# Stages joined without barriers, norm moments merged by group, and the normalising on ScalarE

## The chip, the cores and the metric

The kernel runs on one core of a Trainium2 chip. Its engines are TensorE (PE in the profile, its weight loads PEld), VectorE (DVE), ScalarE (ACT), GpSimd (POOL) and SyncE (SP), which issues DMAs. Each works through its own instructions in order and waits on semaphores for the others. The metric is the device time of one execution in microseconds (us).

## The reference

The input is x of 2048 tokens by 128 channels. Eight residual steps follow each other, and each first applies a layer norm without weights:

```
x = x + attn_softmax(_layernorm(x))      # 16 heads of 8, causal
x = x + channel_mix(_layernorm(x))       # sigmoid(xr Wr) * (relu(xk Wk)^2 Wv)
x = x + gated_linear(_layernorm(x))      # kv_t = k_t * kv_(t-1) + (1 - k_t) * v_t
x = x + channel_mix(_layernorm(x))       # the same weights again
x = x + retention(_layernorm(x))         # fixed decay for each head, group norm, Wo
x = x + experts(_layernorm(x))           # 8 experts, top 2
x = x + lightning(_layernorm(x))         # fixed decay, layer norm, gate, Wo
x = x + experts(_layernorm(x))

def _layernorm(x, axis=-1, eps=1e-05):
    m = jnp.mean(x, axis=axis, keepdims=True)
    v = jnp.var(x, axis=axis, keepdims=True)
    return (x - m) / jnp.sqrt(v + eps)
```

In channel mixing xr and xk are mixtures of a token with the one ahead of it.

## The kernel before

x stays in SBUF as 16 tiles of 128 tokens by 128 channels. Four tiles are a group or chunk of 512 tokens (NC = 4 chunks of TPC = 4 tiles). Normed tiles are transposed on TensorE and copied to xT, channels by tokens, which the products read.

**Order of work.** Every engine's instructions are written out by hand and run in that order; there is no scheduler. Each stage is an nc.Block, and a barrier of all engines lies between two Blocks. The program is: the attention, project_out, channel_mix "f0", linear_attention "g" (gated), channel_mix "f1", end_stage, linear_attention "r" with retention_out, experts "m0", linear_attention "l" with lightning_out, end_stage, experts "m1". end_stage is a Block of its own in which GpSimd clears the semaphores, so that two barriers lie around it.

**Norm.** VectorE takes statistics of each tile of x (bn_stats, L201) as soon as the tile's sum is ready, in the stage ahead. At the start of the next stage seven small VectorE operations merge them for all 16 tiles (L159 to L165), GpSimd raises the variances to the power -1/2, one instruction for each group (L178), VectorE normalises four tiles for each group (L170), TensorE transposes them (L189), and ScalarE copies them out of PSUM (L196). TensorE first issues 12 products whose result nobody reads (unread, L136).

**Channel mixing.** For each chunk GpSimd takes the difference with the shifted tokens (L968), VectorE forms xk and xr (L948, L950), TensorE multiplies (L1000, L1005, L992), ScalarE applies relu, square and sigmoid (L977 to L981), and VectorE gates the product, adds it to x and takes the statistics (L957, L960, L201). TensorE ends with 12 more unread products.

**Linear attention.** 32 steps n, eight for each chunk c, e = n % 8. In a step TensorE spreads the values over the rows (L1269) or a DMA does it, an update is formed on VectorE (L1139) or, in 9 of the steps, on GpSimd (L1109), VectorE scans the recurrence (L1156), GpSimd multiplies the state by q (L1104), and TensorE sums the result four steps later (L1249, L1254). ScalarE takes k and q for each chunk, and in "lightning" it also applies silu to each value (L1207). In "gated" VectorE adds a finished chunk to x in the next one (L1115, L1117), otherwise ScalarE copies it (L1172) and VectorE takes its statistics.

**Experts.** After the norm the gate's logits are made (L1721) and copied (L1536); a long VectorE chain sorts the tokens, and a loop of 39 tiles follows. At the end VectorE adds the weighted results to x, chunk by chunk.

## Time and profile before

| | us |
|---|---|
| median of three runs | 1173.02 |
| lowest and highest run | 1171.45, 1174.34 |
| the profiled execution | 1179.64 |
| its span in the trace | 1177.9 |

Busy time in the span: TensorE 1009.3 us, VectorE 808.1, ScalarE 510.3, GpSimd 432.2. The attention takes the first 491 us. The stages behind it follow each other in the trace: output product from 491.5, f0 from 500.4, g from 527.4, f1 from 605.1, r from 633.5, its output from 704.9, m0 from 718.0, l from 899.6, its output from 978.7, m1 from 997.0.

A row of a timeline reads: start in us, duration in us, engine, line, operation, output and input with their shapes, count, and in brackets how long the engine had stood idle before it and what ended that. Rows of one group that follow each other at once are merged, and the duration is then of all of them. A row of busy time by stretch reads: stretch, its length, then for TensorE, its weight loads, VectorE, ScalarE and GpSimd the busy us and the count, then TensorE's granted clock (1.00 is 2.4 GHz, 0.50 is 1.2 GHz), the DMA share and GB/s.

### The profile page before, as it was taken

The page shows a single profiled execution, that of the slowest core. Times are in us where ns is not written, and L with a number is a line of the kernel's source. Part 1 is how long each engine was busy: PE and PEld are TensorE (multiplying, and loading weights), DVE is VectorE, ACT ScalarE, POOL GpSimd, SP SyncE. Part 2 cuts the span into 40 slices and gives each one's busy share as a digit, 9 for nine tenths or more (in the row PEclk, how much of TensorE's full clock was granted, in tenths as well). Part 3 has the DMA queues.
Part 4 walks back from the last instruction along what each step waited for, and adds up shares of the span by engine and source line. Part 5 has one row for each costly group of instructions (what it writes and reads, how often), then busy time and mean ns, then how long its engine had stood idle before and what let it go on. Part 6 is the DMA issues. An engine that isn't in the chain of part 4 may idle for free. (4 is left out here: it accounts for less than half of the span.)

```text
span 1177.9 us, 18330 instructions
## 1 busy us (share of the span) xinstructions
PE 1009.3 (86%) x6327; PEld 523.2 (44%) x6327; DVE 808.1 (69%) x1504; ACT 510.3 (43%) x1048; POOL 432.2 (37%) x506
## 2 busy tenths in 40 slices
PE   5587899999999999879868976899994996799993
PEld 3232322322222332456645424566662664566662
DVE  6886989999889780288987976533337786733335
ACT  5344577588777677532113102133334431133333
POOL 3320110011011111137862871266652785156661
PEclk9598999999999899979979997999996997899997
DMA  6753500000000000242100201011112210111114
GB/s 127 173 97 55 108 2 2 1 2 2 1 1 2 2 2 2 95 125 70 52 1 10 80 18 36 14 43 42 44 36 81 63 36 1 36 39 41 43 41 122
DMA packets 50207, 51.50 MB, mean 44 GB/s; under 512 B 7668, under 2 KB 39804, under 8 KB 50108
## 3 DMA queue, kind: packets, MB, share of 16 engines
q1 hardware_dynamic: 45128, 40.11, 13.7%
q0 software_dynamic: 4992, 10.23, 3.2%
q8 instruction: 54, 0.88, 0.3%
q14 instruction: 33, 0.27, 0.1%
HBM read 33.22 MB, written 16.91 MB: 43 GB/s over the span
## 5 line engine op out<-in xcount | busy, mean ns | idle before, releaser
L731 DVE TENSOR_REDUCE mpart<-ps 128x2 f32<-128x1024 f32 (+3 forms) x320 | 324.7, 1061 | 48.0 <-PE ps L782 30.6
L859 ACT ACTIVATE arena<-ps 128x512 f32<-128x512 f32 (+3 forms) x640 | 291.7, 542 | 133.1 <-PE ps L799 132.6
L799 PE MATMUL ps<-arena 51*128 51x512 bf16 (+3 forms) x640 | 175.6, 357 | 13.2 <-DMA arena<-mrow 5.8
L813 PE MATMUL ps<-arena,w 128*32 128x512 f32 (+3 forms) x1280 | 154.2, 554 | 2.7 <-ACT arena L859 2.2
L782 PE MATMUL ps<-arena 51*128 51x512 bf16 (+3 forms) x640 | 141.7, 361 | 13.2 <-DVE mpart L731 5.8
L701 POOL TENSOR_SCALAR_AFFINE_SELECT arena<-arena 128x512 f32<-128x512 f32 x64 | 40.8, 637 | 300.1 <-ACT arena L859 230.1
L1697 ACT ACTIVATE arena<-ps 128x512 f32<-128x512 f32 x78 | 46.6, 598 | 214.7 <-PE ps L1763 200.2
L1104 POOL TENSOR_TENSOR arena<-arena 128x512 f32<-128x512 f32 x96 | 121.1, 1274 | 42.4 <-DVE arena L1156 42.1
L799 PEld LDWEIGHTS ps<-arena 51*128 51x128 bf16 x640 | 49.3, 94 | 167.5 <-ACT arena L859 131.1
L1156 DVE TENSOR_TENSOR_SCAN arena<-ps,arena 128x512 f32<-128x512 f32 x96 | 118.3, 1253 | 0.4 <-POOL arena L1109 0.4
L1607 DVE COPY arena<-ps 128x128 f32<-128x128 f32 x78 | 22.8, 292 | 135.8 <-PE ps L1753 96.9
L1662 POOL DMA_INDIRECT results<-arena x78 | 77.2, 989 | 88.5 <-DVE arena L1624 77.8
L1651 POOL DMA_INDIRECT arena<-tokens,arena x78 | 75.9, 973 | 75.1 <-DVE arena L1600 52.0
L136 PE MATMUL ps<-cstb 128*128 128x320 bf16 x324 | 57.9, 344 | 39.2 <-PEq L1491 18.4
L1762 PE MATMUL ps<-w,arena 128*128 x156 | 81.7, 605 | 3.1 <-DVE arena L1607 2.6
L1781 PE MATMUL ps<-w,arena 128*128 x624 | 82.7, 275 | 1.1 <-DVE arena L1624 1.1
L1763 PE MATMUL ps<-w,arena 128*128 x156 | 79.7, 592 | 0.0
L1781 PEld LDWEIGHTS ps<-w,arena 128*128 128x128 f32 x624 | 75.8, 192 | 1.6 <-issue 1.5
L1269 PE MATMUL ps<-xt,arena 128*128 128x512 f32 x138 | 70.4, 598 | 0.7 <-DVE arena L1139 0.7
L178 POOL TENSOR_TENSOR small<-small,neghalf 128x4 f32<-128x4 f32 x32 | 32.5, 1054 | 95.0 <-DVE small L165 95.0
L1139 DVE TENSOR_TENSOR arena<-ps,arena 128x512 f32<-128x512 f32 x69 | 46.7, 678 | 25.6 <-ACT ps L1207 13.4
L196 ACT COPY xt<-ps 128x512 f32<-128x512 f32 x28 | 16.2, 591 | 110.6 <-PE ps L189 110.5
(267 smaller groups left out, 1479.4 us busy)
## 6 DMA issues: line engine op xcount, KB each, us to landing
w<-in_w SPq DMA_DIRECT2D x2, 2048.0 KB, 10.9
arena<-results SPq DMA_DIRECT2D x16, 256.0 KB, 5.0
arena<-q_stack SPq DMA_DIRECT2D x8, 384.0 KB
arena<-k_stack SPq DMA_DIRECT2D x8, 384.0 KB
arena<-g_v SPq DMA_DIRECT2D x9, 256.0 KB, 3.9
arena<-r_v SPq DMA_DIRECT2D x9, 256.0 KB, 3.6
arena<-l_v SPq DMA_DIRECT2D x9, 256.0 KB, 3.6
tokens<-arena SPq DMA_DIRECT2D x8, 256.0 KB, 2.4
```

The source lines that it names most:

```text
L731: nc.vector.tensor_reduce(out=mpart[:, 2 * pl:2 * pl + 2, t, kc], in_=ps[:, bank:bank + 2, 0:width], axis=AX.X, op=ALU.max).then_inc(ring_ ...
L782: ins = nc.tensor.matmul(ps[:, bank + side, 0:width], rows(Qs, side, 2 * g + pl, (c * TPC + t) * P, (c * TPC + t + 1) * P), rows(Ks, side, ...
L799: nc.tensor.matmul(ps[:, n % ST, off:CH], rows(Ks, j % 2, 2 * g + j // 2, kt * P, (kt + 1) * P), rows(Qs, j % 2, 2 * g + j // 2, c * CH + ...
L813: ins = nc.tensor.matmul(ps[32 * j:32 * j + 32, O, off:CH], vg[kt // (NT // 2)][:, kt % (NT // 2), g * GH + j, :], probs[:, u % 2, j, off: ...
L859: nc.scalar.activation(probs[:, n % 2, j[0], off:CH], ps[:, (GH * n + j[0]) % ST, off:CH], ACT.Exp, scale=float(HD) ** -0.5).then_inc(exp_ ...
L1104: nc.gpsimd.tensor_tensor(z[:, n % ZB, :], state[:, n % SB, :], q[:, c % 2, :], ALU.mult).then_inc(z_ready, 1)
L1156: nc.vector.tensor_tensor_scan(out=state[:, n % SB, :], data0=a, data1=upd[n % UB], initial=0.0 if c == 0 else state[:, (n - HD) % SB, CH ...
L1651: nc.gpsimd.indirect_dma_start(out=xs[:, s, :], out_offset=None, in_=token_rows, in_offset=bass.IndirectOffsetOnAxis(ap=gather_row[:, s:s ...
L1662: nc.gpsimd.indirect_dma_start(out=result_rows, out_offset=bass.IndirectOffsetOnAxis(ap=result_row[:, s:s + 1], axis=0), in_=y[:, s % YB, ...
L1762: nc.tensor.matmul(ps[:, i % 2, :], xsT[:, i % 2, :], w1[:, expert[i], :], start=True, stop=True)
L1763: nc.tensor.matmul(ps[:, 2 + i % 2, :], xsT[:, i % 2, :], w3[:, expert[i], :], start=True, stop=True).then_inc(up_ready, 1)
L1781: ins = nc.tensor.matmul(ps[:, 7, 0:D], hidT[:, s % 2, f, :], w2[:, expert[s], f, :], start=f == 0, stop=f == NF - 1)
```

## The change

All that follows the attention is written as Stage objects, which run joins into two Blocks: the first from project_out to retention_out, the second from experts "m0" to experts "m1". One end_stage lies ahead of the first Block, one between the two. Inside a Block each engine goes on with its part of the next stage.

- The merge of the moments is done for each group of four tiles (merge), by VectorE in the stage ahead, right behind the statistics of that group (x_statistics with the norm that follows). Only for "m0" all four merges stand at its own start. In the gated loop the statistics of a chunk now stand right behind its add.
- GpSimd makes power and product of minus mean and power for a group (two instructions), and ScalarE normalises with them (normalise), in one queue with its copies: normalise 0, normalise 1, copy 0, normalise 2, copy 1, normalise 3, copy 2, copy 3.
- In linear attention group 3 is normalised, transposed and copied within step 2 of the recurrence. GpSimd's copies of the weights stand between the powers of groups 1 and 2. Transposes use the banks 1, 5, 1, 7.
- The unread products ahead of each norm and at the end of channel mixing are gone. Those in the experts stay.
- In lightning_out the sigmoids of the gate stand behind the normalising of groups 0 to 2, and that of group 3 between them.

```diff
+            def merge(self, dve, g):
+                if self.link is None:
+                    self.link = Chain(dve, self.chain)
+                link, o = self.link, slice(4 * g, 4 * g + 4)
...
+            def gpsimd(self, pool, groups):
+                for g in groups:
+                    o = slice(4 * g, 4 * g + 4)
+                    pool.wait_ge(self.var_ready, g + 1)
+                    nc.gpsimd.tensor_tensor(small[:, 5, o], small[:, 4, o], neghalf[:, 0:4], ALU.pow).then_inc(self.powered, 1)
+                    pool.wait_ge(self.powered, g + 1)
+                    nc.gpsimd.tensor_tensor(small[:, 6, o], small[:, 0, o], small[:, 5, o], ALU.mult).then_inc(self.rstd_ready, 1)
+
+            def normalise(self, act, g):
+                act.wait_ge(self.rstd_ready, g + 1)
+                for t in range(4 * g, 4 * g + 4):
+                    ins = nc.scalar.activation(self.dst[:, t, :], self.src[:, t, :], ACT.Identity, bias=small[:, 6, t:t + 1],
+                                               scale=small[:, 5, t:t + 1])
+                ins.then_inc(self.normed, 1)
...
-            def tensor(self, pe, groups=None):
-                if groups is None or groups[0] == 0:
-                    unread(self.banks[1], 12)
...
+                last = statistics(range(c * TPC, (c + 1) * TPC), x)
+                if norm is None:
+                    return
+                last.then_inc(norm.chain, 1)
+                norm.link = norm.link or Chain(dve, norm.chain)
+                norm.link.n += 1
+                dve.wait_ge(norm.chain, norm.link.n)
+                norm.merge(dve, c)
...
-                    value(NC - 1)
-                    unread(0, 12)
...
+                    if n == 2:
+                        norm.normalise(act, 3)
+                        norm.copy(act, 3)
...
+            def scalar(act):
+                for g in (0, 1, 2):
+                    norm.normalise(act, g)
+                for c in range(NC):
+                    if c == 2:
+                        norm.normalise(act, 3)
+                    o = slice(c * CH, (c + 1) * CH)
+                    nc.scalar.activation(gate[:, o], gate[:, o], ACT.Sigmoid).then_inc(gate_ready, 1)
...
+        run([attended, mixed, gated, mixed_again, retained, retention_out("r", y, z, None)])
         end_stage()
...
+        run([chosen, lightened, lightened_out, chosen_again])
```

VectorE, from the last chunk of f0's mixing to the first scans of "g", in the kernel before:

```order
L957 TENSOR_TENSOR arena<-ps,arena 128x512
L960 TENSOR_TENSOR x<-arena,x 128x512
L201 BN_STATS stats<-x 128x6 x4
L941 UNCONDITIONAL_BRANCH
L1127 UNCONDITIONAL_BRANCH
L159 TENSOR_TENSOR small<-stats 128x16
L160 TENSOR_TENSOR small<-stats 128x16
L161 TENSOR_TENSOR small<-stats 128x16
L162 TENSOR_TENSOR small<-small 128x16
L163 TENSOR_SCALAR small<-small 128x16
L164 TENSOR_SCALAR small<-small 128x16
L165 SCALAR_TENSOR_TENSOR small<-small 128x16
```

The same place in the changed kernel, where L974 and L977 are what L957 and L960 were:

```order
L974 TENSOR_TENSOR arena<-ps,arena 128x512
L977 TENSOR_TENSOR x<-arena,x 128x512
L212 BN_STATS stats<-x 128x6 x4
L161 TENSOR_TENSOR small<-stats 128x4
L162 TENSOR_TENSOR small<-stats 128x4
L163 TENSOR_TENSOR small<-stats 128x4
L164 TENSOR_TENSOR small<-small 128x4
L165 TENSOR_SCALAR small<-small 128x4
L166 TENSOR_SCALAR small<-small 128x4
L167 SCALAR_TENSOR_TENSOR small<-small 128x4
L1156 TENSOR_TENSOR arena<-ps,arena 128x512 x2
L1173 SCALAR_TENSOR_TENSOR arena<-ps,arena 128x512
```

The seven operations stand behind every group's statistics, three times more within the mixing, and the normalising is gone from VectorE; the updates follow at once.

ScalarE, from the end of f1's mixing into the retention recurrence, before (L977 to L981 are the mixing, L196 the norm's copies, L1187 and L1195 k and q, L1212 the values for the DMA):

```order
L977 ACTIVATE arena<-ps 128x512
L979 ACTIVATE arena<-arena 128x512
L981 ACTIVATE arena<-ps 128x512
L941 UNCONDITIONAL_BRANCH
L1174 UNCONDITIONAL_BRANCH
L196 COPY xt<-ps 128x512 x2
L1187 COPY arena<-ps 128x512
L1195 ACTIVATE arena<-ps 128x512
L196 COPY xt<-ps 128x512 x2
L1212 ACTIVATE xn<-ps 128x512
```

And in the changed kernel (L181 normalises a tile, L197 copies):

```order
L998 ACTIVATE arena<-ps 128x512
L181 ACTIVATE xn<-x,small 128x128 x8
L197 COPY xt<-ps 128x512
L181 ACTIVATE xn<-x,small 128x128 x4
L197 COPY xt<-ps 128x512
L1204 COPY arena<-ps 128x512
L1212 ACTIVATE arena<-ps 128x512
L197 COPY xt<-ps 128x512
L1236 ACTIVATE xn<-ps 128x512
L181 ACTIVATE xn<-x,small 128x128 x4
L197 COPY xt<-ps 128x512
```

Twelve tiles are now normalised ahead of k and q, and four more in the recurrence, behind the first copy of values.

TensorE at the same border, before (L1000, L1005 and L992 are the mixing, L136 the unread products, L189 transposes, L1238 k and q, L1269 and L1277 values):

```order
L992 MATMUL ps<-w_wv,arena 128x128 x8
L136 MATMUL ps<-cstb 128x320 x12
L941 UNCONDITIONAL_BRANCH
L1227 UNCONDITIONAL_BRANCH
L136 MATMUL ps<-cstb 128x320 x12
L189 MATMUL ps<-cst,xn 128x128 x8
L1238 MATMUL ps<-xt,w_rk 128x512
L1238 MATMUL ps<-xt,w_rq 128x512
L189 MATMUL ps<-cst,xn 128x128 x8
L1269 MATMUL ps<-xt,arena 128x512 x2
```

And in the changed kernel:

```order
L1008 MATMUL ps<-w_wv,arena 128x128 x8
L192 MATMUL ps<-cst,xn 128x128 x8
L1266 MATMUL ps<-xt,w_rk 128x512
L1266 MATMUL ps<-xt,w_rq 128x512
L192 MATMUL ps<-cst,xn 128x128 x4
L1299 MATMUL ps<-xt,arena 128x512 x2
L1307 MATMUL ps<-xt,w_rv 128x512
```

The unread products are gone from both sides of the border, and the transposes of the last group come later.

## Rows read from the trace of the kernel before

**Rows 1.** Busy time by stretch, the lightning recurrence from its fourth step.

```profile
916.00:977.50 61.50, 58.68 (x313) 38.98 (x311) 48.28 (x60) 20.82 (x36) 48.10 (x39) 1.00 0.13 39
```

**Rows 2.** Timelines of VectorE, GpSimd and ScalarE, prologue of the attention.

```profile
3.78 0.87 DVE L472 BATCH_NORM_STATS2 xstats<-x 128x6 f32<-128x128 f32 x4 [2.82 <-DMA x<-in_x]
...
9.84 0.86 DVE L472 BATCH_NORM_STATS2 xstats<-x 128x6 f32<-128x128 f32 x4
...
11.51 0.87 DVE L472 BATCH_NORM_STATS2 xstats<-x 128x6 f32<-128x128 f32 x4
...
5.64 1.04 POOL L432 TENSOR_TENSOR small<-small,neghalf 128x4 f32<-128x4 f32 x1 [5.13 <-DVE small L466]
...
6.99 1.65 ACT L584 ACTIVATE xn<-x,small 128x128 f32<-128x128 f32 x4 [4.90 <-POOL small L434]
```

**Rows 3.** Timeline, VectorE's first add of the attention's output product.

```profile
494.03 0.69 DVE L918 TENSOR_TENSOR x<-ps,x 128x512 f32<-128x512 f32 x1 [2.83 <-PE ps L900]
```

**Rows 4.** Timeline, norm and first channel mixing.

```profile
504.88 4.07 DVE L170 TENSOR_SCALAR xn<-x,small 128x128 f32<-128x128 f32 x7
...
510.32 2.08 PE L1000 MATMUL ps<-arena,w_wk 128*128 128x512 f32 x2 [0.20 <-DVE arena L950]
...
516.96 0.69 DVE L957 TENSOR_TENSOR arena<-ps,arena 128x512 f32<-128x512 f32 x1 [1.91 <-PE ps L992]
...
523.70 0.87 DVE L201 BATCH_NORM_STATS2 stats<-x 128x6 f32<-128x128 f32 x4
...
524.50 0.67 DVE L957 TENSOR_TENSOR arena<-ps,arena 128x512 f32<-128x512 f32 x1
```

**Rows 5.** Timeline, gated linear attention: start, third scan, a wait.

```profile
532.75 2.08 POOL L1097 COPY arena<-w_hv 128x128 f32<-128x128 f32 x8
...
540.99 1.21 DVE L1156 TENSOR_TENSOR_SCAN arena<-ps,arena 128x512 f32<-128x512 f32 x1
...
577.21 0.69 DVE L1139 TENSOR_TENSOR arena<-ps,arena 128x512 f32<-128x512 f32 x1 [1.73 <-PE ps L1269]
```

**Rows 6.** Timeline, gated end, second mixing, end_stage, third retention scan.

```profile
602.43 0.69 DVE L1115 TENSOR_TENSOR x<-ps,x 128x512 f32<-128x512 f32 x1 [2.80 <-PE ps L1254]
...
615.00 2.07 PE L1000 MATMUL ps<-arena,w_wk 128*128 128x512 f32 x2 [0.21 <-DVE arena L950]
...
622.20 0.69 DVE L957 TENSOR_TENSOR arena<-ps,arena 128x512 f32<-128x512 f32 x1 [2.47 <-PE ps L992]
...
633.55 0.19 DVE L159 TENSOR_TENSOR small<-stats 128x16 f32<-128x16 f32 x1 [1.52 <-PEq L74]
...
646.97 1.21 DVE L1156 TENSOR_TENSOR_SCAN arena<-ps,arena 128x512 f32<-128x512 f32 x1
```

**Rows 7.** Timeline, start of the first experts.

```profile
718.00 0.17 DVE L1494 MEMSET arena<- 128x128 f32 x1 [0.36 <-PEq L1335]
...
720.65 4.22 DVE L170 TENSOR_SCALAR arena<-x,small 128x128 f32<-128x128 f32 x16 [1.13 <-POOL small L178]
...
727.89 0.69 DVE L1536 COPY arena<-ps 128x512 f32<-128x512 f32 x1 [2.92 <-PE ps L1721]
```

**Rows 8.** Timeline, lightning recurrence: third scan, GpSimd's last products.

```profile
914.31 1.21 DVE L1156 TENSOR_TENSOR_SCAN arena<-ps,arena 128x512 f32<-128x512 f32 x1
...
971.97 3.71 POOL L1104 TENSOR_TENSOR arena<-arena 128x512 f32<-128x512 f32 x3
```

**Rows 9.** Timeline, lightning output and start of the second experts.

```profile
976.93 0.59 ACT L1172 COPY arena<-ps 128x512 f32<-128x512 f32 x1 [8.31 <-PE ps L1254]
...
978.69 1.28 ACT L1412 ACT_TABLE_LOAD   x1 [1.17 <-PEq L1089]
...
1006.95 0.69 DVE L1536 COPY arena<-ps 128x512 f32<-128x512 f32 x1 [2.94 <-PE ps L1721]
```

**Rows 10.** Busy time by stretch, TensorE's clock at the second mixing's start.

```profile
605.00:607.00 2.00, 1.79 (x12) 1.10 (x12) 0.89 (x7) 0.00 (x0) 0.90 (x1) 1.00 0.00 0
...
610.00:613.00 3.00, 1.13 (x5) 0.71 (x4) 3.00 (x5) 1.18 (x2) 3.00 (x4) 0.50 0.00 0
```

More of the change, by code:

```diff
@@ L185, in tensor @@
+            def normalise(self, act, g):
[4 more added lines that the diff above has]
+                ins.then_inc(self.normed, 1)
+            def tensor(self, pe, groups=range(4)):
+                for g in groups:
                     pe.wait_ge(self.normed, g + 1)
[L186 to L187 removed]
+                    before = [h for h in range(g) if self.banks[h] == self.banks[g]]
+                    if before:
+                        pe.wait_ge(self.out, before[-1] + 1)
@@ new lines, in tensor @@
+            def tensor(pe):
+                norm.tensor(pe)
+                for c in range(NC):
+                    pe.wait_ge(gated, c + 1)
+                    if c >= 2:
+                        pe.wait_ge(added, c - 1)
+                    for t in range(TPC):
+                        ins = nc.tensor.matmul(ps[:, 2 + c % 2, t * P:(t + 1) * P],
+                                               xT[:, c * CH + t * P:c * CH + (t + 1) * P], w["lo"][:], start=True, stop=True)
+                    ins.then_inc(product, 1)
@@ L1437, in experts @@
+            return Stage(vector=vector, scalar=scalar, gpsimd=gpsimd, tensor=tensor)
+        def experts(name, token_rows, result_rows, norm, following):
+            last = following is None
             at = [0]
@@ L1785, in build @@
+                    for stage in stages:
+                        if stage.sync:
+                            stage.sync(sp)
         softmax_attention()
-        channel_mix("f0")
-        linear_attention("g", "gated")
-        channel_mix("f1")
         end_stage()
-        linear_attention("r", "retention")
-        experts("m0", tokens[0], results[0], last=False)
-        linear_attention("l", "lightning")
-        end_stage()
-        experts("m1", tokens[1], results[1], last=True)
+        LINEAR_BANKS = (1, 5, 1, 7)
```

1378 lines of the change are left out of this document (689 added, 689 removed).

## The prediction

> **What bounds the kernel now.** I read the timeline around each border of stages first, then the busy time by stretch, then the lines of the long loops. The change does not touch the attention, which fills the first 491 us, nor the long expert loops; it touches six borders and three recurrences. At a border no engine is full. Work passes from one to the next: VectorE's last add and statistics, the merge of the moments, GpSimd's power, a normalising engine, TensorE's transposes, ScalarE's copy. So a border is priced by the length of that chain, and a queue that one engine is in order by. The barriers themselves are small: VectorE stands 0.36 us at a plain one and 1.52 us where end_stage lies between two [rows 6, 7]. In the lightning recurrence TensorE is busy 58.7 of 61.5 us and VectorE 48.3, GpSimd 48.1 [rows 1]; in the gated one VectorE has a wait of up to 1.73 us once in a chunk of some 16 us [rows 5].
>
> **Prices of the new pieces.** The prologue of the attention already works in the new way, by groups of four tiles [rows 2]. VectorE's statistics begin at 9.84 and the next ones at 11.51: 1.67 us with a merge. In channel mixing the next operation starts 0.80 us after the statistics [rows 4]. A merge so costs VectorE 0.87 us for each group, where before one merge of about the same length did for 16 tiles. From the start of the statistics to the power it is 1.86 us (3.78 to 5.64), from the power to ScalarE 1.35 us (5.64 to 6.99; power and product on GpSimd), and ScalarE takes 1.65 us for four tiles. VectorE took 4.2 us for 16 [rows 7], so the normalising itself gets 2.4 us longer per norm, and it is in ScalarE's queue with the 0.6 us copies.
>
> **Border 1: output product, first channel mixing, gated start.** VectorE's adds begin at 494.03 [rows 3]; a group is then 0.73 + 0.80 + 0.87 = 2.40 us, the last power can start at 494.03 + 0.73 + 1.86 + 3 x 2.40 = 503.8, ScalarE normalises from 505.2 to 506.85, and transposes at 1.1 us let TensorE start the mixing at 508.0. Before it started at 510.32. From there to the first gated product it was 6.64 us (516.96) and I keep that, since ScalarE's table load and the low clock stay: 514.65. Then VectorE sets the pace, 0.72 + 0.73 + 0.80 + 0.87 = 3.1 us a group which is longer than what TensorE needs between two products there [rows 4]: powers from 517.95, 521.1, 524.2, 527.35. The gated start needs group 1 normalised (522.45 to 524.1) and copied (524.7); GpSimd puts 2.1 us of weight copies [rows 5] between the powers of groups 1 and 2, so ScalarE normalises group 2 till 527.8, copies, and makes decay and k (1.3 us) by about 529.7. TensorE's value products for steps 0 to 2 follow; that of step 3 stands behind the transposes of group 3, which wait for ScalarE's normalising in the loop. The third scan comes at 536.2 with a fast TensorE, 537.6 with a slow one, before 540.99 [rows 5]. With 1.2 us for the end_stage that now stands behind the attention: a gain of 2.7 us, bounds 1 to 4.
>
> **Gated loop.** Three merges (2.6 us) and one set of statistics (0.8 us) come into the loop, on VectorE's way. One wait of 1.73 us per chunk can swallow part [rows 5]. Loss 3.0 us, bounds 1.5 (half is swallowed) and 5 (TensorE and GpSimd stall behind it).
>
> **Border 2: gated end, second mixing, retention start.** TensorE's last products let VectorE add at 602.43 [rows 6]. By then groups 0 and 1 are nearly normalised; the last power starts at 602.43 + 0.73 + 0.73 + 1.86 = 605.75, and behind GpSimd's first difference at 606.6; ScalarE normalises group 3 from 608.0 to 609.65, transposes till 610.8. Before it was 615.00: 4.2 us. The first gated product comes 7.2 us later as before (622.20 to 618.0). Powers at 621.3, 624.4, 627.6, 630.7; end_stage is gone. The third scan, by the same steps as above, at 639 to 640.5, before 646.97. Gain 7.3, bounds 5 to 8.5.
>
> **Border 3: retention output, experts start.** The barrier ahead of the output gives 0.3 us back; end_stage costs 1.2 us more than the plain barrier did. From the first memset (718.00) to the copy of the logits it was 9.9 us [rows 7]. Now: 0.7 us to the first merge, power at 1.7, ScalarE from 3.0; normalise, normalise, copy, normalise, copy, normalise, copy, copy are 4 x 1.65 + 4 x 0.6 = 9.0 us in one queue, with a wait for the last transposes 9.6, then the logits 1.2: 13.8. Loss 3.9 + 1.0 = 4.9, bounds 3.5 and 5.3. What hid this before was that VectorE and ScalarE shared it.
>
> **Border 4: experts to lightning.** The tail of the experts is VectorE's: 4 merges of 0.87 less one end merge and a barrier. Power of the last group 2.6 us later than before, but the early groups are long normalised: scans could start 2.4 us sooner. Yet in step 2 ScalarE must normalise and copy group 3 (2.3 us) ahead of the value of step 3, and the third scan comes at 914.7 against 914.31 [rows 8]. Loss 0.3, bounds -1 and +1.
>
> **Lightning loop.** Three merges, 2.6 us, in a loop where VectorE has 13 us of waits [rows 1]. But the last merge stands ahead of the last scan while GpSimd works 3.71 us in a row [rows 8]. In the first mixing seven normalising operations took VectorE 4.07 us beside GpSimd's differences [rows 4], against 0.26 us each without them. If the merge waits in this way for two such operations, the last scan slips by 2.1 us, and the two before it by some 0.5 each. Loss 3.0, bounds 1 and 5. The Trainium skill, page "SBUF — State Buffer", section "Who interferes with whom", says that a VectorE instruction with two SBUF inputs contends with a GpSimd instruction that reads SBUF; statistics, with one input, do not. The trace agrees for the slow operations just named, and shows none of a merge in such a place; by the rule the merge pays, without it the loss is 1.
>
> **Border 5: lightning output, experts start.** ScalarE is free at 977.5 [rows 9]: three normalisings, a table load of 1.28, two sigmoids, the fourth normalising: 986.4; transposes and the scale and shift till 987.9, then the first product: VectorE's add at 989.65. Powers at 992.25 + 3 x 2.40 = 999.45, ScalarE 1000.8 to 1002.45, transposes and copy 1004.1, logits 1005.2. Before 1006.95 [rows 9]. Gain 1.8, bounds 0.5 and 3.5.
>
> **Sum.** 2.7 - 3.0 + 7.3 - 4.9 - 0.3 - 3.0 + 1.8 = +0.6 us gained. The profiled execution took 1179.64 us (span 1177.9), 6.6 over the median of the three timed runs; from 1179.64 to 1179.0, and on the median 1173.02 to 1172.4.
>
> **TensorE's clock.** The filler matmuls ahead of every norm and after each mixing are gone. They worked only partly: from 605 to 607 the filler had the clock at 1.00, from 610 to 613, after sparse transposes, it was 0.50, thus 1.2 GHz, and the first products of the mixing, 1.0 us each, ran so too [rows 6, 10]. A mixing so already starts slow, and my terms carry that. What is new is that the starts of the recurrences, which had it at 1.00 after 24 fillers, come after sparse transposes too. The Trainium skill, page "TensorE: Matmul & The Clock Gate", section "Why this matters for your kernels", advises against idle gaps between bursts; by it the change would lose, and the third rival prices that from rows.
>
> **Rivals.**
> First, *the cover holds* (faster): merges vanish in the waits of the loops (loop losses 1.5 and 1.0), and TensorE is fast at the borders (gains 3.5, 8.2, 2.8, losses 4.8 and 0.3). Sum 7.9: 1165. For it: VectorE's 13 us of waits. Against it: the place of the last merge.
> Second, *merges collide with GpSimd* (slower): each of six merges in loops waits for two operations of 1.25 us; the loops lose 5 + 5 instead of 6: 1176.5. It decides the sign when loops lose more than 8.2 us with the borders as above.
> Third, *the clock falls further* (slower): a product takes 2.07 us at 1.2 GHz [rows 6], some 1.0 us more than at 2.4. If one more chunk of three products runs so in each mixing, that is 3.1 us less about 0.5 of VectorE's surplus, twice 2.6; and each of three recurrence starts waits one such product more, with its transposes 1.3 us: 5.2 + 3.9 = 9.1 us, 1181.5. For it: clocks of 0.50 after sparse transposes. Against it: at 605 the clock was still 1.00 though TensorE had had nothing since 602.4 [rows 6, 10].
> That the change doesn't do what it says can be left out: its order shows the pieces.
>
> **How the numbers follow.** The forecast, 1172.4 with own range 1168 to 1177, has 0.40; the first rival 0.30; the second 0.13; the third 0.17. The range 1163.5 to 1181 leaves some 0.15 out. A difference under 0.3% (3.5 us) can't be told from none. Faster by more: nearly all of the first rival and a fifth of the forecast, 0.37. Slower by more: most of the third, three quarters of the second, a tenth of the forecast, 0.28. Within: 0.35.
>
> **What would show it.** In the new profile: a VectorE group of mixing at 3.1 us; the first scan of retention 8 us sooner relative to the gated end; 13.8 us from the experts' memset to the logits; the two loops longer by 3 us each; GpSimd's wait ahead of the last two products of lightning. I would be wrong if the clock in the mixings is at 1.00 from the start or at 0.50 throughout, or if a merge in a loop takes over 1.5 us or costs its loop nothing.

## The result, and the profile after

The changed kernel takes 1178.87 us (median of five runs, 1178.35 to 1180.21), the kernel before 1173.02 (five runs, 1171.45 to 1174.78). The ratio is 1.0051, 95% interval 1.0037 to 1.0066: slower by 5.9 us, where 0.6 us less was forecast. When the changed kernel was measured once more beside other runs of the kernel before, the ratio was 1.0036 (1.0014 to 1.0059).

The profiled execution took 1179.97 us, its span is 1178.2. Only 0.3 us separate it from the span of before, since the attention, which is the same code in both, ended 4.1 us earlier in it (VectorE's last operation there starts at 486.80 against 490.92). Over all the executions profiled for this study that time lies anywhere from 482.6 to 490.9. So the traces are compared from the attention's end on, and there the changed kernel takes 691.4 us against 687.0: 4.4 us longer. The table cuts these into intervals between starts of VectorE rows.

| interval | before | after | gained | forecast |
|---|---|---|---|---|
| attention's end to first add of the output product | 3.11 | 3.88 | -0.8 | -1.2 |
| first add to third gated scan | 46.96 | 41.95 | +5.0 | +3.9 |
| third gated scan to gated end (last add) | 61.44 | 67.76 | -6.3 | -3.0 |
| gated end to third retention scan | 44.54 | 36.15 | +8.4 | +7.3 |
| third retention scan to group norm | 57.93 | 58.25 | -0.3 | 0 |
| group norm to first memset of the experts | 13.10 | 14.34 | -1.2 | -1.0 |
| memset to copy of the logits | 9.89 | 14.09 | -4.2 | -3.9 |
| logits to first weighted add, first experts | 160.16 | 159.11 | +1.1 | 0 |
| weighted add to third lightning scan | 26.26 | 27.33 | -1.1 | -0.3 |
| third to fifth lightning scan | 3.86 | 6.62 | -2.8 | 0 |
| fifth lightning scan to last statistics | 59.38 | 63.38 | -4.0 | -3.0 |
| last statistics to logits of the second experts | 29.40 | 28.17 | +1.2 | +1.8 |
| logits to end of span | 170.95 | 170.37 | +0.6 | 0 |

Timeline of VectorE in the changed kernel: first add, first gated product, third gated scan, one operation of a merge in the gated loop, the loop's wait, an operation of the last merge in the loop, last gated add, first gated product of the second mixing, third retention scan, memset and copy of the logits at the experts.

```profile
490.68 0.69 DVE L937 TENSOR_TENSOR x<-ps,x 128x512 f32<-128x512 f32 x1 [3.58 <-PE ps L921]
...
511.27 0.69 DVE L974 TENSOR_TENSOR arena<-ps,arena 128x512 f32<-128x512 f32 x1 [1.55 <-PE ps L1008]
...
532.63 1.21 DVE L1173 TENSOR_TENSOR_SCAN arena<-ps,arena 128x512 f32<-128x512 f32 x1
...
558.13 0.16 DVE L162 TENSOR_TENSOR small<-stats 128x4 f32<-128x4 f32 x1
...
571.31 0.69 DVE L1156 TENSOR_TENSOR arena<-ps,arena 128x512 f32<-128x512 f32 x1 [1.74 <-PE ps L1299]
...
592.34 1.23 DVE L163 TENSOR_TENSOR small<-stats 128x4 f32<-128x4 f32 x1
...
600.39 0.69 DVE L1130 TENSOR_TENSOR x<-ps,x 128x512 f32<-128x512 f32 x1 [3.88 <-PE ps L1282]
...
615.82 0.69 DVE L974 TENSOR_TENSOR arena<-ps,arena 128x512 f32<-128x512 f32 x1 [2.76 <-PE ps L1008]
...
636.54 1.21 DVE L1173 TENSOR_TENSOR_SCAN arena<-ps,arena 128x512 f32<-128x512 f32 x1
...
709.13 0.17 DVE L1518 MEMSET arena<- 128x128 f32 x1 [1.56 <-PEq L74]
...
723.22 0.69 DVE L1562 COPY arena<-ps 128x512 f32<-128x512 f32 x1 [10.07 <-PE ps L1743]
```

These answer to [rows 3 to 7]. Borders 1 and 2 are what the steps said, or better, and border 3 is 0.5 us worse. The gated loop is far off: its wait of 1.73 us [rows 5] is still there, 1.74 us, so it has swallowed nothing of the new operations. TensorE's rows ahead of it in the changed kernel (L1282 sums, L1299 gives the value):

```profile
567.53 1.16 PE L1282 MATMUL ps<-arena 128*128 128x128 f32 x8 [1.29 <-POOL arena L1120]
...
570.25 1.02 PE L1299 MATMUL ps<-xt,arena 128*128 128x512 f32 x2
```

The value that VectorE waits for stands in TensorE's order behind sums that waited 1.29 us for GpSimd, and GpSimd multiplies what VectorE has scanned. The three engines take turns: when VectorE comes later, so do the others, and the wait is no slack.

Timelines of TensorE and VectorE at the start of the lightning recurrence in the changed kernel, and TensorE's busy time by stretch there (the sixth figure behind the length is the granted clock):

```profile
906.38 0.66 PE L192 MATMUL ps<-cst,xn 128*128 128x128 f32 x4 [2.21 <-ACT xn L181]
906.87 1.53 PE L1299 MATMUL ps<-xt,arena 128*128 128x512 f32 x2
908.33 2.07 PE L1316 MATMUL ps<-arena,w_lg 8*128 8x512 f32 x2
910.33 2.08 PE L1299 MATMUL ps<-xt,arena 128*128 128x512 f32 x2
```

```profile
904.47 1.21 DVE L1173 TENSOR_TENSOR_SCAN arena<-ps,arena 128x512 f32<-128x512 f32 x1
909.05 0.69 DVE L1156 TENSOR_TENSOR arena<-ps,arena 128x512 f32<-128x512 f32 x1 [3.37 <-ACT ps L1231]
909.66 1.21 DVE L1173 TENSOR_TENSOR_SCAN arena<-ps,arena 128x512 f32<-128x512 f32 x1
913.06 0.69 DVE L1156 TENSOR_TENSOR arena<-ps,arena 128x512 f32<-128x512 f32 x1 [2.19 <-ACT ps L1231]
```

```profile
904.00:907.00 3.00, 0.79 (x6) 0.62 (x6) 1.68 (x2) 2.12 (x5) 2.28 (x2) 1.00 0.24 76
907.00:910.00 3.00, 3.00 (x5) 0.56 (x3) 0.95 (x2) 1.17 (x2) 0.02 (x1) 0.54 0.58 193
910.00:913.00 3.00, 3.00 (x7) 1.64 (x7) 0.87 (x1) 1.14 (x2) 1.27 (x1) 0.50 0.00 0
```

TensorE stands idle for 2.21 us in front of the four transposes of group 3, which wait for ScalarE's normalising. Behind them come the values of step 3, which have nothing to do with group 3. Then the granted clock falls from 1.00 to 0.50, 1.2 GHz, and a value product, which is two rows of the trace, takes 2.08 us instead of 1.02. VectorE waits 3.37 and 2.19 us.

Timeline of VectorE at the end of the lightning loop in the kernel before, where the last scan began 0.77 us behind the start of the statistics:

```profile
971.92 0.85 DVE L201 BATCH_NORM_STATS2 stats<-arena 128x6 f32<-128x128 f32 x4
972.69 1.26 DVE L1156 TENSOR_TENSOR_SCAN arena<-ps,arena 128x512 f32<-128x512 f32 x1
```

And in the changed kernel, where it begins 3.11 us behind:

```profile
972.06 0.85 DVE L212 BATCH_NORM_STATS2 stats<-arena 128x6 f32<-128x128 f32 x4
972.94 0.44 DVE L161 TENSOR_TENSOR small<-stats 128x4 f32<-128x4 f32 x1
973.31 1.30 DVE L162 TENSOR_TENSOR small<-stats 128x4 f32<-128x4 f32 x1
...
975.17 1.28 DVE L1173 TENSOR_TENSOR_SCAN arena<-ps,arena 128x512 f32<-128x512 f32 x1
```

And GpSimd's rows at the same place, and at the merge at 592.34 of the gated loop:

```profile
592.28 1.26 POOL L1120 TENSOR_TENSOR arena<-arena 128x512 f32<-128x512 f32 x1
...
972.10 2.49 POOL L1120 TENSOR_TENSOR arena<-arena 128x512 f32<-128x512 f32 x2
```

An operation of four columns takes 1.23 or 1.30 us beside a GpSimd product of 1.25, and 0.16 without one (558.13 above). The last merge meets two products: its first operation, 0.44 us, ends with the first of them, its second with the second. The two earlier merges of the lightning loop have one operation each of 0.63 and 0.62 us; two of the three in the gated loop meet none.

### The profile page after: what moved, and what is told of

Read it like the earlier page. It is cut to its first block and busy times, and to the rows that moved or that the text cites. A ratio compares the mean times of both kernels' runs of the same rounds, so it can differ in the third digit from the quotient of the medians.

```text
span 1178.2 us, 18204 instructions
## 1 busy us (share of the span) xinstructions
PE 992.3 (84%) x6207; PEld 512.7 (44%) x6207; DVE 795.5 (68%) x1544; ACT 558.7 (47%) x1176; POOL 439.6 (37%) x538
## 5 line engine op out<-in xcount | busy, mean ns | idle before, releaser
L824 PEld LDWEIGHTS ps<-arena 51*128 51x128 bf16 x640 | 49.3, 94 | 166.6 <-ACT arena L884 131.9
L1299 PE MATMUL ps<-xt,arena 128*128 128x512 f32 x138 | 72.3, 612 | 6.0 <-DVE arena L1156 6.0
L807 PEld LDWEIGHTS ps<-arena 51*128 51x128 bf16 x640 | 36.1, 94 | 56.4 <-DVE mpart L756 38.3
L192 PE MATMUL ps<-cst,xn 128*128 128x128 f32 x96 | 21.0, 357 | 45.9 <-ACT xn L181 45.9
```

The lines of the kernel that those rows point to most:

```text
L807: ins = nc.tensor.matmul(ps[:, bank + side, 0:width], rows(Qs, side, 2 * g + pl, (c * TPC + t) * P, (c * TPC + t + 1) * P), rows(Ks, side, ...
L824: nc.tensor.matmul(ps[:, n % ST, off:CH], rows(Ks, j % 2, 2 * g + j // 2, kt * P, (kt + 1) * P), rows(Qs, j % 2, 2 * g + j // 2, c * CH + ...
```

## The experiments

The theory after this reading: the loss is in the recurrences, from work on VectorE's way in two loops, and from group 3's norm standing in step 2. The rivals: the clock alone, for want of the unread products, or something that the joined borders cost. Each ratio is to the kernel before on the same chip, whose median was 1174.2 to 1174.8 us in these runs, so a thousandth is 1.17 us. Differences to the changed kernel are taken from its first ratio, 1.0051; from its second, 1.0036, each gain would be 1.8 us smaller.

### Group 3 later

```diff
-                    if n == 2:
-                        norm.normalise(act, 3)
-                        norm.copy(act, 3)
+                    if n in (3, 4, 6, 7):
+                        norm.normalise_tile(act, 3, (3, 4, 6, 7).index(n))
+                    if n == HD + 1:
+                        norm.copy(act, 3)
...
-                    if n == 2:
+                    if n == HD:
                         norm.tensor(pe, (3,))
```

> The changed kernel, but in all three recurrences the last group of tokens is normalised by ScalarE one tile at a time in steps 3, 4, 6 and 7, transposed by TensorE in step 8 and copied in step 9, instead of all in step 2. Group 3 is first read in step 17. Theory (TensorE, in order, is held at the four transposes of step 2 and then works at the low clock): the fifth lightning scan comes 30.5 us after the experts' first weighted add instead of 33.95 as in the changed kernel (before: 30.1), the starts of the gated and the retention recurrence each gain 0.6 us, median 4.7 us under the changed kernel, 1174.2. Rival (the starts are slow because the unread products are gone, whatever stands in step 2): the lightning products stay at 1.0 us each, a gain of at most 1 us, 1178.

Measured: 1173.1 us, ratio 0.9986 (0.9973 to 0.9999), 7.6 us under the changed kernel, where 4.7 were expected; behind the attention the trace is 5.5 us shorter. Timeline of VectorE at the lightning start:

```profile
901.06 1.21 DVE L1181 TENSOR_TENSOR_SCAN arena<-ps,arena 128x512 f32<-128x512 f32 x1
...
905.06 1.21 DVE L1181 TENSOR_TENSOR_SCAN arena<-ps,arena 128x512 f32<-128x512 f32 x1
...
908.91 1.21 DVE L1181 TENSOR_TENSOR_SCAN arena<-ps,arena 128x512 f32<-128x512 f32 x1
```

First, third and fifth scan are 4.00 and 3.85 us apart, as before (4.00 and 3.86), and the fifth comes 28.0 us behind the experts' weighted add: not only back from 33.95 but ahead of the 30.1 of before. The early merges do bring 2.1 us at this border, and step 2 had eaten them. From the mixings' first gated products on, the gated start gains 1.2 us and the retention start 0.6. ScalarE's tiles inside the loop cost 0.45 us. Ahead of the first mixing's first gated product, where the edit changes nothing, this execution is 0.9 us longer. The rival is refuted: there is no unread product in the norms of this kernel, and its lightning products are as fast as before.

### Merges behind the loops

```diff
+                if c >= 1:
+                    dve.wait_ge(x_added, c)
+                    last = statistics(range((c - 1) * TPC, c * TPC), x)
+                    if c == NC - 1:
+                        merge_after(dve, last, following, range(NC - 1))
                 dve.wait_ge(z_used, (c + 1) * HD)
...
+                if kind == "lightning" and c == NC - 1:
+                    dve.wait_ge(measured, NC - 1)
+                    following.link = Chain(dve, following.chain)
+                    for g in range(NC - 1):
+                        following.merge(dve, g)
                 dve.wait_ge(sum_out, c + 1)
```

> The changed kernel, but in the gated and the lightning recurrence the merges of groups 0 to 2 stand behind the last scan, where VectorE waits 3.9 and 3.2 us for TensorE's last sums, and the gated statistics stand one chunk later again, as before. Theory (VectorE is the bound of both loops, so each merge and each set of statistics in them is paid in full, and the one near the end more than that, beside GpSimd): the gated loop from its ninth scan to the last add is 5.0 to 5.7 us shorter, the lightning one from the fifth scan to the last statistics 3.5 to 4 us, median 1170 to 1171. Rival (the lightning loop is TensorE's, and longer for another reason, such as the slow start): only the gated loop gains 5 us, 1174.

Measured: 1168.66 us, ratio 0.9946 (0.9930 to 0.9962), 12 us under the changed kernel. From the ninth to the last gated scan it is 45.9 us instead of 51.3, from the fifth to the last lightning scan 54.5 instead of 58.9: both as before. The merges behind the lightning loop cost 0.6 us of that again up to the last statistics, those behind the gated loop nothing. The theory on the loops is shown, in both of them. Timeline of VectorE at the gated end: behind the three merges the last add starts without a wait, where it waited 3.88 us in the changed kernel.

```profile
592.10 0.84 DVE L212 BATCH_NORM_STATS2 stats<-x 128x6 f32<-128x128 f32 x4
592.97 0.62 DVE L161 TENSOR_TENSOR small<-stats 128x4 f32<-128x4 f32 x1
...
595.78 0.68 DVE L1144 TENSOR_TENSOR x<-ps,x 128x512 f32<-128x512 f32 x1
```

That makes 5.7 us in the gated loop and 3.7 in the lightning one; another 2.8 are from a place that the edit does not touch, third to fifth lightning scan, 3.86 us here. Timeline of TensorE there, and its busy time by stretch:

```profile
902.75 0.66 PE L192 MATMUL ps<-cst,xn 128*128 128x128 f32 x4 [2.21 <-ACT xn L181]
903.24 1.02 PE L1321 MATMUL ps<-xt,arena 128*128 128x512 f32 x2
904.19 1.12 PE L1338 MATMUL ps<-arena,w_lg 8*128 8x512 f32 x2
```

```profile
905.00:908.00 3.00, 3.00 (x14) 1.80 (x14) 2.71 (x4) 1.17 (x2) 1.19 (x1) 1.00 0.24 65
```

The same instructions with the same gap of 2.21 us, and the clock stayed at 1.00. First to third scan are still 6.67 us apart, not 4.00. This parts the two costs of the lightning start: 2.7 us for the wait in order, 3.3 for the clock where it falls.

### Unread products in the gap

```diff
                     if n == 2:
+                        if kind == "lightning":
+                            unread(7, 8)
                         norm.tensor(pe, (3,))
```

> The changed kernel with eight unread products (128x320, about 0.28 us each at full clock) in the lightning recurrence, right ahead of the transposes of group 3 in step 2, where TensorE stood idle for 2.2 us. Theory A (the clock that fell in this gap is most of the slow start): the products behind it run at the granted clock of 1.00, value products of 1.0 us for two instead of 1.5 to 2.1, and the fifth scan comes 2.5 us sooner, 1176.4. Theory B (the wait in order itself is the cost): the products are fast but the fifth scan gains under 1 us, 1178 to 1179.

Measured: 1178.26 us, ratio 1.0036 (1.0024 to 1.0048), 1.8 us under the first ratio of the changed kernel and the same as its second. The eight products took 1.26 us together and left 1.02 us of the gap. In the trace the products behind the gap are fast, and the two intervals (first to third, third to fifth scan) 6.68 and 3.86 us: theory A by the trace, 3.3 us, of which the medians show 1.8 or nothing. Since the run before shows the same intervals without these products, one trace doesn't prove that they did it.

### The first experts' norm on VectorE

```diff
+                if on_vector:
+                    for g in range(NC):
+                        dve.wait_ge(norm.rstd_ready, g + 1)
+                        for t in range(4 * g, 4 * g + 4):
+                            ins = nc.vector.tensor_scalar(norm.dst[:, t, :], norm.src[:, t, :], small[:, 0, t:t + 1],
+                                                          small[:, 5, t:t + 1], ALU.add, ALU.mult)
+                        ins.then_inc(norm.normed, 1)
```

> The changed kernel with the norm of the first experts normalised by VectorE, which has nothing else to do there, and ScalarE only copying. Theory (ScalarE's one queue of normalising and copies is the cost at this border): memset to logits copy 9.5 to 10 us instead of 14.1, median 1174.5 to 1175. Rival (the chain from merge to power to product and TensorE's low clock hold the border): 12 us and 1177.

Measured: 1178.7 us, ratio 1.0044 (1.0027 to 1.0061): 0.8 us, where 4 were expected. A miss. Memset to logits is 12.48 us, 1.6 of the 4.2 us back. Timelines of VectorE and TensorE, and the clock:

```profile
712.12 0.17 DVE L1519 MEMSET arena<- 128x128 f32 x1 [1.56 <-PEq L74]
...
719.61 1.12 DVE L1535 TENSOR_SCALAR arena<-x,small 128x128 f32<-128x128 f32 x4 [0.49 <-POOL small L176]
...
724.60 0.69 DVE L1570 COPY arena<-ps 128x512 f32<-128x512 f32 x1 [3.79 <-PE ps L1755]
```

```profile
717.12 3.17 PE L192 MATMUL ps<-cst,arena 128*128 128x128 f32 x12 [9.20 <-DVE arena L1535]
```

```profile
722.00:724.00 2.00, 2.00 (x8) 0.20 (x5) 0.00 (x0) 1.80 (x2) 0.00 (x0) 0.50 0.29 84
```

VectorE now does all four merges ahead of its normalising and then waits for GpSimd's last power. The normalising ends 8.6 us behind the memset, 1.7 later than before [rows 7], and TensorE works at 0.50 up to the logits. So this run puts another cost in the place of ScalarE's queue and does not price the queue. The changed kernel's own rows do (ScalarE's last normalising, and the gate's products):

```profile
717.72 1.65 ACT L181 ACTIVATE arena<-x,small 128x128 f32<-128x128 f32 x4
...
720.48 2.63 PE L1743 MATMUL ps<-xt,arena 128*32 128x512 f32 x8
```

There the normalising ends 10.2 us behind the memset, 3.4 later than the 6.9 of before, and only 0.4 of that is a later start. The other 0.8 of the 4.2 us stands behind it, where the gate's products take 2.63 us at the low clock, and 1.79 before.

### Unread products in every norm

```diff
                     if before:
                         pe.wait_ge(self.out, before[-1] + 1)
+                    if g >= 1:
+                        unread(self.banks[g], 5)
+                    pe.wait_ge(self.normed, g + 1)
```

> The changed kernel with five unread products (128x320) ahead of TensorE's wait for each of groups 1 to 3 in every norm; between two groups TensorE has 1.4 to 2.5 us of idle time. Theory A (the sparse transposes let the clock fall to 0.50 and the first products of both mixings and of the experts' gate run at 1.2 GHz for that reason alone): the first gated product comes 1.5 to 2 us sooner behind the output product (20.6 us) and behind the gated end (15.4 us), and 4 to 5 us go in all, 1175. Theory B (the products are as slow as the clock that they find: 0.55 us each at 0.50, five are 2.7 us and delay the transposes): the borders get up to 1 us longer each, 1180 to 1184.

Measured: 1172.69 us, ratio 0.9989 (0.9977 to 1.0001): 7.3 us under the changed kernel, more than theory A said, and theory B is refuted: five products in a row took 0.84 us at the second mixing. Timeline of TensorE at the second mixing's start in this kernel, and its busy time by stretch:

```profile
608.62 0.66 PE L194 MATMUL ps<-cst,xn 128*128 128x128 f32 x4 [2.08 <-ACT xn L181]
609.12 1.02 PE L1018 MATMUL ps<-arena,w_wk 128*128 128x512 f32 x2
```

```profile
607.00:610.00 3.00, 1.38 (x7) 0.90 (x8) 1.41 (x2) 2.63 (x6) 1.76 (x2) 1.00 0.02 5
```

The same two views of the changed kernel:

```profile
607.91 1.11 PE L192 MATMUL ps<-cst,xn 128*128 128x128 f32 x4 [2.30 <-ACT xn L181]
608.82 1.91 PE L1016 MATMUL ps<-arena,w_wk 128*128 128x512 f32 x2
```

```profile
606.00:609.00 3.00, 1.09 (x5) 1.09 (x6) 1.41 (x2) 2.12 (x5) 1.76 (x3) 0.50 0.00 0
```

The gain lies 2.7 us in front of the second mixing's gated product, 1.3 each at the first experts and the lightning output, and 3.3 at the lightning start, which two executions without these products had as well (merges behind, above, and barriers back, below); only 0.2 at the first mixing, and 1.2 are lost again ahead of the output product's first add (5.11 us instead of 3.88, as in the execution with VectorE in the experts' norm; why stays open). The expectation missed the experts, the output and the lightning start.

### The kernel before without its unread products

```diff
-                if groups is None or groups[0] == 0:
-                    unread(self.banks[1], 12)
...
                     value(NC - 1)
-                    unread(0, 12)
```

> The kernel before without the unread products ahead of the norms and at the end of the mixings, nothing else changed: the part of the change that the clock rival rests on, alone. Theory (they worked only in part, and the changed kernel's recurrence starts showed the clock at 1.00 without them): 1 to 3 us slower, 1175 to 1177. Rival (they carry the clock across the borders): a chunk more at 1.2 GHz in each mixing and a slow start of three recurrences, 9 us slower, 1183.

Measured: 1176.46 us, ratio 1.0017 (1.0004 to 1.0031): 2.0 us slower, as the theory said. In the kernel before they are worth little; without them its gated and retention starts are 1.5 and 1.3 us longer in the trace. Where they stood, ahead of the first transposes and at the end of the mixings, they brought a quarter of what five of them between the groups bring to the changed kernel.

### Barriers back, and the changed kernel again

```diff
-        run([attended, mixed, gated, mixed_again, retained, retention_out("r", y, z, None)])
+        for stage in (attended, mixed, gated, mixed_again, retained, retention_out("r", y, z, None)):
+            run([stage])
```

and in the same way for the second four stages.

> The changed kernel with each stage in a program of its own, thus with the barriers back between all stages, and everything else (merges by group, ScalarE normalising, order) as changed. Theory (what the joined borders gain is the overlap: powers and normalising of groups 0 to 2 run while VectorE still adds the last groups, and ScalarE's queue of 9 us is only tolerable in that way): from the gated end to the second mixing's first gated product 22 to 24 us instead of 15.4 (before: 19.8), and 4 to 8 us at each of six borders that have a norm, 1178.9 + 30 = 1209. Rival (a barrier costs its own 0.4 us, the rest is the cheaper merge): eight times 0.4 to 0.6, 1182 to 1184.

Measured: 1222.81 us, ratio 1.0415 (1.0391 to 1.0439), 43 us over the changed kernel and 14 over the 1209 of the theory. Gated end to gated product is 19.5 us, 4.0 more than in the changed kernel but less than expected; the retention start lost 8.0, the gated start 7.3, the way from the output product to the first mixing 5.3, the second experts 5.3, the lightning start 7.3 up to its first scan and 4.0 up to the fifth, since here the clock stayed at 1.00. The rival, that a barrier costs only itself, is refuted. Timeline of ScalarE at the second mixing:

```profile
617.47 3.18 ACT L181 ACTIVATE xn<-x,small 128x128 f32<-128x128 f32 x8 [34.04 <-POOL small L176]
...
623.78 1.65 ACT L181 ACTIVATE xn<-x,small 128x128 f32<-128x128 f32 x4 [0.64 <-POOL small L176]
```

ScalarE has been idle for 34 us, though the moments of groups 0 to 2 were merged long before: power, normalising and copies stand behind the barrier and come one after the other. With the barriers in place all the rest of the change (merges by group, ScalarE's queue, group 3 in step 2, no unread products) costs 4%; it is the joined programs that give back most of it.

> The changed kernel itself, once more. In two profiled executions of kernels that have its lightning start (the changed kernel and the one with VectorE in the experts' norm) the products behind TensorE's 2.2 us gap ran at a granted clock of 0.50, and third to fifth scan took 6.6 and 6.9 us; in one with the same gap and the same code there (merges behind) it stayed at 1.00 and they took 3.9. If the outcome is a matter of chance, the segment is one of the two values again, all other segments behind the attention agree with the first execution within 0.3 us, and the median is 1.005 of the kernel before. If the clock falls whenever the gap is there, it is 6.6 again, and the lucky run stands unexplained.

This one has no edit. Measured: 1180.31 us, ratio 1.0036. All intervals agree with those of the first execution within 0.3 us, but for the last, from the logits of the second experts to the end, with 0.7. TensorE at the lightning start again:

```profile
907.44 0.66 PE L192 MATMUL ps<-cst,xn 128*128 128x128 f32 x4 [2.22 <-ACT xn L181]
907.93 1.30 PE L1299 MATMUL ps<-xt,arena 128*128 128x512 f32 x2
909.16 2.07 PE L1316 MATMUL ps<-arena,w_lg 8*128 8x512 f32 x2
```

The clock fell again. It did so in three executions with these instructions (the changed kernel twice, and with VectorE in the experts' norm) and stayed in two (merges behind, barriers back), whose gap was 2.21 us as well. That it is a matter of chance is not shown, and what decides stays open. The two that kept the clock differ in what came earlier: in the three others it had risen to 1.00 between 5.2 and 5.5 us ahead of the first scan, in these 6.7 us (merges behind) and 3.6 us (barriers back). No run varied this by itself.

### Together

> The changed kernel with both edits of the two earlier runs: group 3 spread over steps 3 to 9, and the merges of the gated and lightning loops behind the last scan. If the two causes are separate, their parts add: against the changed kernel 5.4 us in the gated loop, 4.4 in the lightning one, 1.2 and 0.6 at the gated and retention starts and 6.0 at the lightning start, less 0.5 for the normalising inside the loops, thus 17 us, 1163 where the kernel before takes 1174.2. If the low clock of the lightning start was a matter of chance in which the second run was lucky (its start was 2.8 us shorter without any edit there), the sum against the medians of those two runs is 7.0 + 9.5, thus 1163.5; if both edits take the same waits away, 1167.

Measured: 1165.22 us, ratio 0.9906 (0.9886 to 0.9925), 17 us under the changed kernel by the ratios. In the trace the intervals that the edits touch are 17.1 us shorter together, as the sum said: the two causes add.

The next has the norm of the first experts as in the kernel before as well (one merge over 16 tiles, VectorE normalises, twelve unread products).

> As the run with both edits, and with the norm of the first experts exactly as in the kernel before: one merge over 16 tiles, VectorE normalises, ScalarE copies, twelve unread products ahead of the transposes. Theory (three things add up to the 4.2 us at this border: ScalarE's queue 1.6 as the run with VectorE alone showed, four merges for one 1.7, the low clock 0.9): memset to logits copy 9.9 us, and the median 4 us under that of the run with both edits, 1159. Rival (what is gained there is lost to the clock of the sorting behind it): 1161 to 1163.

Measured: 1159.29 us, ratio 0.9870 (0.9855 to 0.9885), 4.2 us less again by the ratios (5.9 by the medians), and memset to logits 10.3 us instead of 14.1. The last adds five unread products ahead of the waits for the groups of the other norms:

> The kernel of the run with all three edits (group 3 late, merges behind the last scan, the first experts' norm as before; 1159.3) with five unread products ahead of TensorE's wait for groups 1 to 3 in the norms of the mixings, of the lightning output and of the second experts, and for groups 1 and 2 of the recurrences. If the 7 us that these products brought to the changed kernel lie at the borders (2.7 us ahead of the second mixing's first gated product, 1.3 at the lightning output) and the rest in the lightning start, which is fast in this kernel anyway, 3 to 4 us are left: 1155.5. If they also shorten runs through the attention or the sorting, which differ from one execution to the next, the full 7: 1152. If they take turns with what the other edits gained: 1159.

Measured: 1153.07 us, ratio 0.9821 (0.9801 to 0.9841): 21 us faster than the kernel before and 27 faster than the changed one. The step from the kernel without them is 5.7 us, between the two expectations. It lies in front of the two mixings' first gated products (0.9 and 1.5 us), at the lightning output (1.3), at the first and the second experts (0.6 and 1.3). Two of these are not shown to be the products' work. The first experts' norm got none in this run. And the 0.9 us at the first mixing are no more than the spread there: without such products the way to it took 20.4 to 20.8 us in five executions of the changed kernel and its variants, and 21.5 in three.

## Why the prediction was wrong

Two steps failed, and together they turn the sign: the gated loop, where a wait was taken for cover (3.3 us), and the start of the lightning recurrence, where the pitch (the time from scan to scan) behind the third scan was taken as unchanged (3.6 us). Borders 1 and 2 gained 2.6 us more than was said, and the remaining intervals lost 0.7 more, so that the trace is 5.0 us off.

**The baseline.** I summed against an execution 6.6 us over the median and kept the difference. That was sound: its attention ended at 490.9 us, the latest of all executions, so the excess lay largely there.

**Border 1** was forecast at +2.7 and is +4.2, just beyond its bounds. VectorE's group of 2.40 us holds to the digit (490.68 and 493.08), the first gated product comes 2.3 us sooner, as worked out, and the group in mixing is 3.13 us (the last one 3.6 to 3.8). The third scan came another 1.1 us sooner, and end_stage cost 0.4 less.

**Gated loop, -3.0, is -6.3**, outside its bounds. The step that failed is that a wait of 1.73 us per chunk "can swallow part" of the new work; it is still 1.74. Each merge and set of statistics is paid, and a collision with GpSimd, which I priced for the lightning loop alone, comes on top. The rows of the loop give 3.4 us for three merges and a set of statistics, 1.1 for one merge operation beside GpSimd, 0.3 for longer adds, some 0.5 since a merge waits for the statistics where another operation would overlap them, 0.6 for group 3 in step 2, and 0.3 at the last sums.

**Border 2, +7.3, is +8.4**, the first gated product 4.3 us sooner where 4.2 was said, and the retention scans sooner by the rest. **Border 3, -4.9, is -5.4**, memset to logits 14.1 against 13.8. The reason given holds: ScalarE's normalising ends 3.4 us later behind the memset than VectorE's did. The near match of the sum is partly luck: ScalarE's last copy ends 12.0 us behind the memset where 12.6 was said, and from there to the logits it is 2.1 us where 1.2 was said, since the gate's products run at the low clock.

**Border 4, -0.3, is -3.9 up to the fifth scan**, the larger of the two failed steps. I worked out the third scan (909.66 is 1.1 us late by the interval, 0.3 was said) and stopped there, as if the pitch of the loop began with it. I had even written that the value of step 3 stands behind the transposes, and had priced ScalarE's 2.3 us but not what TensorE's gap does to the products behind it. At the low clock that is 2.8 us between third and fifth scan and 0.5 ahead of the third; where the clock stayed, the wait in order alone left 2.7 us. With group 3 later the border is worth +2.1, so the price of its place was 6 us.

**Lightning loop, -3.0, is -4.0.** The last merge costs 2.3 us up to the last scan where 2.1 was said. The mechanism is the one named, but that the sizes agree is partly luck: two waits were counted and the merge's own 0.87 us left out, and it is one full wait of 1.1, one of 0.3, and the merge. The two earlier ones cost 0.6 and 1.4 where 0.5 each was said. Of the signs named, a merge of over 1.5 us in a loop, this is one; the last of the gated loop, 1.9 us, is another. The Trainium skill, page "SBUF — State Buffer", section "Who interferes with whom", lets a VectorE instruction with two SBUF inputs contend with a GpSimd instruction that reads SBUF; the trace agrees, at 1.23 and 1.30 us for an operation of 0.16. The normalising that the prediction counted for it reads one tensor and, for its scalars, small, and is no plain case of it. **Border 5, +1.8, is +1.2.**

**The rivals.** The second, that merges collide with GpSimd, gave the loops 10 us and they lost 10.3, which is luck in good part: the six merges met GpSimd for 3.4 us in all (1.1 in the gated loop; 0.5, 0.5 and 1.4 in the lightning one), and the rest was plain work on VectorE's way. Its turning point was put at loops that lose more than 8.2 us, but the terms of the sum give 6.6; either was passed. The first rival's terms add up to 6.9 and not 7.9, thus 1166; it is refuted either way. The third, the clock without unread products, came in at one of three recurrence starts, 3.3 us, and there it needed the gap: with group 3 later the clock stayed, with no unread product in the norms. The first mixing was not slower than before. The Trainium skill, page "TensorE: Matmul & The Clock Gate", section "Why this matters for your kernels", advises against idle gaps between bursts; the run with unread products in the norms agrees in direction, with 7.3 us, though the gaps of 2.2 and 2.3 us in the rows above are shorter than those the page speaks of. The chances were too kind to the cover of waits, for which only a sum of idle time spoke.

## What to carry to other kernels

Before small work is put into a loop for a later stage's sake, ask whether the loop's waits belong to the engine or to a cycle that it closes itself: a wait that its own output ends, through other engines, is no cover. Put the work behind the last iteration, where the engine waits for a drain (here three merges cost nothing behind one loop and 0.6 us behind the other). In an in-order engine price an instruction that is placed early by everything behind it, up to the point where the old pitch is reached again, and place it by when its result is first read (here step 17, not step 2). Taking barriers out can be worth far more than their own length once per-group work is ready to run across them.

## What the runs showed of the hardware

- The same gap of 2.21 us on TensorE was followed by a granted clock of 0.50 in three executions and of 1.00 in two, with the same instructions right around it. The outcome is worth 3.3 us here.
- At the second mixing's start, filler products between sparse transposes kept the clock at 1.00 where twelve of them ahead of the first transpose had not (0.50) [rows 10]. Five for each group were worth 7.3 us in one kernel and 5.7 in another, not all of it at places where they stood or are shown to have acted.
- A VectorE operation on 128x4 with two inputs from SBUF took 1.23 to 1.30 us where it was issued at the start of a GpSimd product of 1.25 us, 0.44 to 0.63 where it came later in one, and 0.16 alone.
- The attention, the same code in every kernel here, ended between 482.6 and 490.9 us of its trace. A difference of a few us between two spans says nothing before that part is taken out.
